# Adding the experts' weighted rows to the tokens' rows in HBM by accumulating indirect transfers, instead of storing them and gathering them back

## The chip, the cores and the metric

The kernel runs on one core of one Trainium2 chip. The metric is the device time of one execution in microseconds (us). All operands are float32.

## What is computed

Two layers of a gated decoder work on `x`, four sequences of 512 tokens with 512 features (2048 tokens). Each layer adds a state-space block and then a feed-forward block, both behind a tanh gate. The feed-forward block of the first layer is a mixture of 16 experts, of which each token takes 4, with weights. That block and how its rows meet again is what the change touches:

```python
x = x + tanh(g_xattn[0]) * ssm0(ctx, layernorm(x), ...)
x = x + tanh(g_ffn[0]) * moe(layernorm(x), ...)         # this block
x = x + tanh(g_xattn[1]) * ssm1(ctx, layernorm(x), ...)
x = x + tanh(g_ffn[1]) * lora_ffn(layernorm(x), ...)

def moe(x, ...):                       # x: 2048 tokens x 512
    w, sel = route(x)                  # 4 of 16 experts a token, weights sum to 2.5
    for each expert e:
        y = silu(x @ gate[e].T) * (x @ up[e].T) @ down[e].T      # inner size 256
        out += cw[:, e, None] * y      # cw is zero where e was not selected
    return out + shared_expert(x)
```

The scan of the state-space block reads only `ctx` and weights, not `x`; `x` enters it at the end, as the gate `silu(layernorm(x))`. So the scans of layer 2 can run while the experts of layer 1 are at work, and that is what the kernel does.

## The kernel before

**Stages.** The eight scans (two layers of four sequences) are stages s = 0 to 7. A stage has 32 units (16 states by two halves of the 512 channels). One unit is a multiplication on DVE (`mul_b`, L1498, which writes PSUM), a scan on DVE (`scan`, L1506), a multiplication by C on GpSimd (`mul_c`, L433) and a sum. In stages 0 to 4 TensorE sums the units in PSUM (L974). In stages 5 to 7 TensorE has the experts, and DVE sums (`add_y`, L1517), two units after the scan. `mul_c` of a unit starts only when `mul_b` of the next one is done, so that it lies beside the scan.

**Turns.** Stages 5 to 7 are cut into 48 turns of two units (an even and an odd one), and turn m carries one tile of tokens, with one lag for each step. The 8192 pairs of token and expert are sorted by expert into 79 chunks (`NCH`) of 128 rows. A tile has two chunks of the same expert or one: 32 full tiles and 15 half ones, 47 (`NTILE`). In turn m GpSimd issues the gathers of tile m + 2 after the even `mul_c` (`gather_rows`, L475, one indirect transfer of 128 rows of 2 KB for each chunk, from `xn_d`). SP issues the loads of the B and C rows (L293, 512 KB), the expert's weights of tile m + 1 (`load_tile_w`, L312, 1.5 MB; it first waits until tile m - 1 has left TensorE, as there are two slots) and the store of tile m - 1 (`store_tile`, L318) into `ys_d`, an array in HBM with a row for each pair. TensorE runs tile m - 1: the gate and up products (L1054), the next tile's transposes (L1033), the down product (L1065). ACT forms the tanh (L715) and copies the result out of PSUM (`tile_out`, L722) into the one buffer `YSB`, for which it waits on the store of the tile before. DVE forms the hidden rows (`tile_hidden`, L1524 and L1527) before `add_y` and before `scan` of the even unit.

**Routing.** In stage 4 DVE ranks the experts and works out each pair's slot (`slots`). Then eight rounds turn slots into an index of rows: ACT marks the row of each pair (`mark_rows`, L676 and L682), DVE marks its chunk (`mark_chunks`, L1490), and TensorE multiplies the marks (`index_round`, L1041), which leaves in PSUM, for each slot, the number of its token. DVE copies that to `IDX` (L1633). The slots, as integers (`SLU`), and the weights (`CWK`) are kept for the tail.

**Tail.** When the last unit is summed, GpSimd gathers the four expert rows of each token from `ys_d` (L520, 64 indirect transfers, 16 for each sequence b), and DVE adds them with their weights to `X` (`combine`, L1680, 16 instructions for each sequence). Then for each sequence: statistics (L1299), the gate (L627, L1309), transposes and the sum (L984, L1323), statistics again, the normalised rows (L636), their transposes (L993), the router of the second feed-forward (L1225), its gates on DVE (L1690 to L1716), the base product (L1195, three of four blocks ahead of the transposes L1208, one behind L984), the LoRA product (L1217) and the last sum (`lora_add`, L1725). Sequence b is begun before sequence b - 1 is finished: on DVE the order is combine(b), statistics(b), logits and gates of b - 1, gate and sum of b, `lora_add`(b - 1). GpSimd adds the bias of b - 1 (L510) meanwhile.

The waits that matter for the order stand in these lines:

```python
dve.wait_ge(gathered[q], 16 * TOPK * (b + 1))     # combine
pe.wait_ge(x_final, QT * l)                       # base(l, ...) behind lora_add(l - 1)
pool.wait_ge(ys_stored, 16 * NTILE)               # the tail's gathers behind all stores
```

## Time and profile before

| | |
|---|---|
| median of 3 runs | 1691.06 us (1689.95 to 1692.73) |
| the profiled execution | 1696.96 us, its span 1695.2 us |
| PE busy | 1259.6 us, 74% |
| PE weight loads | 694.2 us, 41% |
| DVE busy | 1498.9 us, 88% |
| ACT busy | 823.0 us, 49% |
| GpSimd busy | 874.9 us, 52% |
| DMA | 264.26 MB, of which 37.50 MB on GpSimd's queue |
| stages 5 to 7 with the tiles | about 915 to 1495 us |
| the tail | about 1495 us to the end |

Busy shares are means over stages with different limits, so the table alone does not say what a change is worth. Times in the rows are from the start of the span. "POOL" is GpSimd. A row of the timeline gives start, duration, engine, line, operation, output and input; in square brackets stands how long the engine had been idle and what ended that.

### The profile page before, as it was taken

Reading aid. Unit: us, or ns where it says so; the run is one execution under the profiler, and the core shown is the slowest. Engines: PE = TensorE matmul, PEld = TensorE weight load, DVE = VectorE, ACT = ScalarE, POOL = GpSimd, SP = SyncE. Lnnn points to the kernel's source line nnn. Section 1 sums busy time; section 2 is a strip of 40 time slices with the busy share of each in tenths; the row PEclk is TensorE's granted clock in tenths of the full one; section 3 lists DMA queues with packets and bytes.
Section 4 is the critical chain, followed back from the end, with each engine's and each line's share of the span. In section 5 each row is a group of like instructions: output and inputs, shape, how many; then the busy total and the mean of one; then the engine's idle time right before and its main releaser. Section 6 shows DMA issues by size and latency. Waiting matters only on the chain.

```text
span 1695.2 us, 13647 instructions
## 1 busy us (share of the span) xinstructions
PE 1259.6 (74%) x4084; PEld 694.2 (41%) x4084; DVE 1498.9 (88%) x1511; ACT 823.0 (49%) x1288; POOL 874.9 (52%) x449
## 2 busy tenths in 40 slices
PE   5566576677666876778777998789987899805678
PEld 2122132333233322334343656556665566603344
DVE  3999999899989999999987999899998999967883
ACT  4455537363725363532692666546665444404341
POOL 0357636643663367433245456764557666466521
PEclk7798789789978898898887999989999899956888
DMA  6244435523542354334155777766886788654421
GB/s 224 74 135 124 108 99 143 131 67 107 143 132 60 90 142 115 89 94 125 38 137 137 227 250 265 250 218 214 262 251 205 269 274 265 222 162 122 138 74 50
DMA packets 99834, 264.26 MB, mean 156 GB/s; under 512 B 10832, under 2 KB 11344, under 8 KB 93616
## 3 DMA queue, kind: packets, MB, share of 16 engines
q1 hardware_dynamic: 87936, 225.36, 44.3%
q0 software_dynamic: 11440, 37.50, 6.5%
q8 instruction: 33, 0.54, 0.1%
q10 hardware_dynamic: 384, 0.52, 0.1%
q14 instruction: 41, 0.34, 0.1%
HBM read 233.73 MB, written 29.62 MB: 155 GB/s over the span
## 4 chain that ended last, share of the span: by engine, by line
DVE 22%; PE 18%; issue 8%; DMA 5%; POOL 4%; ACT 4%; SPq 0%; DVEq 0%; ACTq 0%; POOLq 0%
PE banks L1054 8%; DVE state L1506 7%; DVE banks L1498 5%; PE banks L1065 3%; DMA expert_w<-in_moe_w 3%; POOL state L433 2%; DMA ys_d<-expert_out 2%; PE banks L1195 2%; DVE y_scan L1517 2%; DVE x_res L1680 1%; PE banks L1033 1%; DVE du L1265 1%; DVE small L1299 1%; PE banks L974 1%; PE banks L1225 1%
## 5 line engine op out<-in xcount | busy, mean ns | idle before, releaser
L433 POOL TENSOR_TENSOR state<-state,bc_rows 128x1024 f32<-128x1024 f32 x256 | 605.7, 2367 | 673.2 <-DVE banks L1498 673.1
L974 PE MATMUL banks<-state,ident 128*128 128x512 f32 x640 | 366.5, 706 | 194.2 <-POOL state L433 193.9
L1506 DVE TENSOR_TENSOR_SCAN state<-decay,banks 128x1024 f32<-128x1024 f32 x176 | 402.1, 2285 | 9.8 <-ACT decay L658 5.1
L1498 DVE TENSOR_TENSOR banks<-du,bc_rows 128x1024 f32<-128x1024 f32 x256 | 351.6, 1374 | 22.2 <-PE banks L974 8.2
L1054 PE MATMUL banks<-z_gate,expert_w 128*128 128x256 f32 (+1 forms) x1504 | 288.8, 351 | 12.0 <-DMA expert_w<-in_moe_w 6.7
L974 PEld LDWEIGHTS banks<-state,ident 128*128 128x128 f32 x640 | 127.1, 215 | 405.4 <-POOL state L433 289.9
L658 ACT ACTIVATE decay<-delta,neg_a 128x511 f32<-128x511 f32 x352 | 231.2, 713 | 104.8 <-DVE state L1506 51.8
L1054 PEld LDWEIGHTS banks<-z_gate,expert_w 128*128 128x128 f32 x1504 | 252.5, 193 | 67.2 <-issue 25.5
L1506 DVE TENSOR_TENSOR_SCAN state<-expert_w,banks 128x1024 f32<-128x1024 f32 x80 | 182.9, 2286 | 2.8
L1065 PE MATMUL banks<-expert_w,hidden 128*128 128x512 f32 x316 | 159.0, 619 | 2.9 <-DVE hidden L1527 2.9
L1517 DVE TENSOR_TENSOR y_scan<-y_scan,state 128x1024 f32<-128x1024 f32 x96 | 136.2, 1420 | 11.5 <-POOL state L433 11.5
L658 ACT ACTIVATE expert_w<-delta,neg_a 128x511 f32<-128x511 f32 x160 | 103.7, 710 | 15.3 <-DVE state L1506 15.3
L708 ACT ACTIVATE z_gate<-banks 128x512 f32<-128x512 f32 (+1 forms) x94 | 49.4, 526 | 75.8 <-PE banks L1033 74.7
L722 ACT ACTIVATE expert_out<-banks 128x512 f32<-128x512 f32 x79 | 45.5, 596 | 75.5 <-DMA ys_d<-expert_out 58.8
L1013 PE MATMUL banks<-y_scan,expert_w 128*128 128x512 f32 x128 | 68.2, 694 | 8.5 <-DVE hidden L1535 7.3
L1065 PEld LDWEIGHTS banks<-expert_w,hidden 128*128 128x128 f32 x316 | 54.8, 198 | 35.6 <-issue 31.7
L538 ACT ACTIVATE du<-banks,chan 128x512 f32<-128x512 f32 x32 | 23.9, 770 | 92.0 <-PE banks L919 90.7
L984 PE MATMUL banks<-ident,y_scan 128*128 128x128 f32 x128 | 23.6, 342 | 57.6 <-DVE y_scan L1309 52.7
L715 ACT ACTIVATE hidden<-banks 128x256 f32<-128x256 f32 (+1 forms) x94 | 32.3, 343 | 70.2 <-PE banks L1054 70.2
L1021 PE MATMUL banks<-expert_w,hidden 128*128 128x512 f32 x64 | 41.6, 811 | 31.0 <-DVE hidden L1535 31.0
L1195 PE MATMUL banks<-expert_w,du 128*128 128x512 f32 x128 | 58.3, 610 | 0.0
L646 ACT ACTIVATE rstd<-rstd 128x4 f32<-128x4 f32 x16 | 3.3, 205 | 106.3 <-DVE rstd L1304 78.5
(233 smaller groups left out, 1670.8 us busy)
## 6 DMA issues: line engine op xcount, KB each, us to landing
bc_rows<-bc_d SPq DMA_DIRECT2D x208, 512.0 KB, 4.9
expert_w<-in_moe_w SPq DMA_DIRECT2D x48, 1536.0 KB, 9.1
ys_d<-expert_out SPq DMA_DIRECT2D x32, 512.0 KB, 10.3
ctx_t<-in_ctxT SPq DMA_DIRECT2D x8, 512.0 KB, 6.7
x_res<-in_x SPq DMA_DIRECT2D x4, 1024.0 KB, 10.5
xn_d<-y_scan SPq DMA_DIRECT2D x4, 1024.0 KB, 7.5
ys_d<-expert_out SPq DMA_DIRECT2D x15, 256.0 KB, 9.2
out_x<-x_res SPq DMA_DIRECT2D x3, 1024.0 KB, 4.3
```

Of the source, the lines that this page charges most:

```text
L433: nc.gpsimd.tensor_tensor(W[:, c % 4], W[:, c % 4], bcast2(BC[:, u, 1, :]), ALU.mult).then_inc(mulc_done, 1)
L658: ins = nc.scalar.activation(DAS[c % n][:, m, 1:], DEL[:, s % 2, et, 1:], ACT.Exp, scale=AN[:, lay(s), et, state:state + 1])
L708: nc.scalar.activation(XST[:, 2 * h:2 * h + 2, 0:n], XT[:, h, :, 0:n], ACT.Copy).then_inc(xst_ready, 1)
L722: nc.scalar.activation(YSB[:, r, :], out_bank(j, r), ACT.Copy).then_inc(yev, 1)
L974: mm = nc.tensor.matmul(PS[:, m], ID[:, :], W[:, c % 4, m, :], start=False, stop=True, skip_group_check=True)
L1013: mm = nc.tensor.matmul(AUX[g], MW[:, 0, at:at + P], XNT[:, k, :], start=(k == 0), stop=(k == ET - 1))
L1054: mm = nc.tensor.matmul(PS[:, it, g * TILE:g * TILE + n], MW[:, u % 2, at:at + P], XST[:, k, 0:n], start=(k == 0), stop=(k == ET - 1))
L1065: mm = nc.tensor.matmul(out_bank(j, r), HT[:, u % 2, it, r * P:(r + 1) * P], MW[:, u % 2, at:at + D], start=(it == 0), stop=(it == IT - 1))
L1195: nc.tensor.matmul(PS[:, q], xnt[:, k, q * P:(q + 1) * P], BW[:, k, :], start=(k == 0), stop=(k == ET - 1))
L1498: nc.vector.tensor_tensor(drive(s), DU[:, s % 2, 2 * h:2 * h + 2, :], bcast2(BC[:, u, 0, :]), ALU.mult).then_inc(mulb_done, 1)
L1506: nc.vector.tensor_tensor_scan(flat(W[:, c % 4]), flat(DAS[c % da_slots(s, i)]), flat(drive(s)), 0.0, ALU.mult, ALU.add).then_inc(scan_don ...
L1517: nc.vector.tensor_tensor(y, y, W[:, k % 4], ALU.add).then_inc(w_free, 1)
```

## The change

In stages 5 to 7 each finished chunk of an expert is added to an array of the tokens' sums in HBM, and nothing is gathered in the tail.

- A new array `acc_d` in HBM holds `X` (after the shared expert's part) from before the tiles: SP stores each sequence into it (`store_sum`, 1 MB each, four of them, at the ends of stages 2 and 3 and twice in stage 4). `xn_d` and `acc_d` get 256 rows ahead of the tokens' (`SPARE`), filled from `x` at the start (two copies of 512 KB from HBM to HBM), so that empty slots have rows of their own to read and to add to.
- The index product also carries the weights: `mark_chunks` writes for each pair the chunk's mark and the mark times weight over row number, in four instructions instead of one, and the product has 158 columns instead of 79. `read_index` then copies the weights of the slots (`SLOTW`), gives empty slots a spare row (`PLACE`) and forms `IDX`.
- ACT scales each row by its slot's weight as it copies it from PSUM (`tile_out`), into one of two buffers in turn (`YSB` and the first two blocks of `X`, which are free once `X` is in `acc_d`). It waits for the additions of the tile two before, not for the store of the last.
- GpSimd issues `add_rows(m - 2)` after the odd `mul_c` of turn m: an indirect transfer with add for each chunk, from the buffer into `acc_d` at the rows of `IDX`. It first waits for ACT's copies and for all earlier additions to have landed (`added`). The store to `ys_d` is gone from SP's list.
- After the last unit GpSimd issues the additions of the last tile, and SP, when all 79 have landed, loads `acc_d` back into `X`: four loads of 256 KB for the first sequence, then one of 1 MB for each other. The 64 gathers and the 64 instructions of `combine` are gone.

```diff
-        GK = [W[:, 0:2].rearrange("p a b n -> p (a b) n"), W[:, 2:4].rearrange("p a b n -> p (a b) n"),
-              DA[:, :, :, :].rearrange("p a b n -> p (a b) n"),
-              MW[:, 1, 0:QT * D].rearrange("p (q n) -> p q n", q=QT)]
+        OUT = [YSB, X[:, 0:RT]]
...
-        xn_d = nc.dram_tensor("xn_d", (NB * L, D), F32, kind="Internal").ap()
-        ys_d = nc.dram_tensor("ys_d", (NCH * P, D), F32, kind="Internal").ap()
-        ys_c = ys_d.rearrange("(c p) n -> p c n", p=P)
-        xn_t = xn_d.rearrange("(b q p) n -> b p q n", p=P, q=QT)
+
+        xn_d = nc.dram_tensor("xn_d", (SPARE + NB * L, D), F32, kind="Internal").ap()
+        acc_d = nc.dram_tensor("acc_d", (SPARE + NB * L, D), F32, kind="Internal").ap()
+        xn_t, acc_t = [v[SPARE:, :].rearrange("(b q p) n -> b p q n", p=P, q=QT) for v in (xn_d, acc_d)]
...
+            def store_sum(b):
+
+                sp.wait_ge(shacc, QT * (b + 1))
+                sp.dma_start(acc_t[b], X[:, b * QT:(b + 1) * QT, :]).then_inc(acc_stored, 16)
...
+            for rows in (xn_d, acc_d):
+                sp.dma_start(rows[0:SPARE, :], t["x"][0, 0:SPARE, :]).then_inc(spare_stored, 16)
...
+                if s >= 2:
+                    store_sum(s - 2)
...
                     sp.dma_start(xn_t[NB - 1], XN).then_inc(xn_stored, 16)
+                    store_sum(NB - 2)
                 if k == HS - 4:
-                    sp.wait_ge(slots_ready, 2)
+                    store_sum(NB - 1)
+                    sp.wait_ge(slots_ready, 1)
...
-                    if m:
-                        store_tile(m - 1)
...
+            sp.wait_ge(added, 16 * NCH)
+            for q in range(QT):
+                sp.dma_start(X[:, q, :], acc_t[0][:, q, :]).then_inc(acc_first[q], 16)
+            for b in range(1, NB):
+                sp.dma_start(X[:, b * QT:(b + 1) * QT, :], acc_t[b]).then_inc(acc_in[b - 1], 16)
...
+            def add_rows(j):
+
+                pool.wait_ge(yev, DONE[j + 1])
+                if j:
+                    pool.wait_ge(added, 16 * DONE[j])
+                for r in range(BLOCKS[j]):
+                    at = chunk_of(j) + r
+                    nc.gpsimd.indirect_dma_start(
+                        out=acc_d, out_offset=bass.IndirectOffsetOnAxis(ap=IDX[:, at:at + 1], axis=0),
+                        in_=OUT[j % 2][:, r, :], in_offset=None, compute_op=ALU.add).then_inc(added, 16)
...
+                        if m == 0 and c == 0:
+                            pool.wait_ge(acc_stored, 16 * NB)
                         if c % 2 == 0 and m + 2 < NTILE:
                             gather_rows(m + 2)
+                        if c % 2 and m >= 2:
+                            add_rows(m - 2)
...
-            pool.wait_ge(w_free, HS * STAGES + PRE_W)
-            pool.wait_ge(ys_stored, 16 * NTILE)
-            for g in range(NT):
-                b, q = g // QT, g % QT
-                if b:
-                    pool.wait_ge(combined, TOPK * QT * (b - 1) + (TOPK - 1) * QT + q + 1)
-                for k in range(TOPK):
-                    nc.gpsimd.indirect_dma_start(
-                        out=GK[q][:, k, :], out_offset=None, in_=ys_d,
-                        in_offset=bass.IndirectOffsetOnAxis(ap=SLU[:, k, g:g + 1], axis=0)).then_inc(gathered[q], 16)
-                if q == QT - 1 and b:
-                    add_bias(b - 1)
-            add_bias(NB - 1)
+            add_rows(NTILE - 1)
+            for b in range(NB):
+                add_bias(b)
...
             def tile_out(j):
-                if j:
-                    act.wait_ge(ys_stored, j * 16)
+                if j >= 2:
+                    act.wait_ge(added, 16 * DONE[j - 1])
                 for r in range(BLOCKS[j]):
                     act.wait_ge(y_done, DONE[j] + r + 1)
-                    nc.scalar.activation(YSB[:, r, :], out_bank(j, r), ACT.Copy).then_inc(yev, 1)
+                    at = chunk_of(j) + r
+                    nc.scalar.activation(OUT[j % 2][:, r, :], out_bank(j, r), ACT.Copy, scale=SLOTW[:, at:at + 1]
+                                         ).then_inc(yev, 1)
...
-                    mm = nc.tensor.matmul(INDEX, ROWHOT[n % 3][:, c, :], CHUNKHOT[n % 3][:, c // TOPK, c % TOPK, :],
+                    mm = nc.tensor.matmul(INDEX, ROWHOT[n % 3][:, c, :], flat(CHUNKHOT[2 * (n % 3) + c // TOPK][:, c % TOPK]),
...
-                row = COUNT1[:, 0:NCH].unsqueeze(1).unsqueeze(1)
-                shape = [P, PPR // TOPK, TOPK, NCH]
-                nc.vector.tensor_tensor(CHUNKHOT[n % 3], row.to_broadcast(shape), own.unsqueeze(3).to_broadcast(shape),
-                                        ALU.is_equal).then_inc(chunkhot, 1)
+                row = COUNT1[:, 0:NCH].unsqueeze(1).to_broadcast([P, TOPK, NCH])
+                over_j = lambda v: v.unsqueeze(2).to_broadcast([P, TOPK, NCH])
+                of_group = lambda v, g: v.rearrange("p (k t) -> p t k", k=TOPK)[:, g, :]
+                for a in range(PPR // TOPK):
+                    hot, g = CHUNKHOT[2 * (n % 3) + a], PPR // TOPK * n + a
+                    ins = nc.vector.tensor_tensor(hot[:, :, 0, :], row, over_j(of_group(CHUNK1, g)), ALU.is_equal)
+                link(ins)
+                for a in range(PPR // TOPK):
+                    hot, g = CHUNKHOT[2 * (n % 3) + a], PPR // TOPK * n + a
+                    ins = nc.vector.tensor_tensor(hot[:, :, 1, :], hot[:, :, 0, :], over_j(of_group(SHARE, g)), ALU.mult)
+                ins.then_inc(chunkhot, 1)
+
+            def read_index():
+
+                dve.wait_ge(indexed, ROUNDS)
+                nc.vector.tensor_copy(SLOTW[:, :], INDEX[:, NCH:])
+                empty = T2[:, 0:NCH]
+                for r in range(RT):
+                    ins = nc.vector.tensor_scalar(empty[:, r::RT], INDEX[:, r:NCH:RT], 0.0, PLACE[:, r:r + 1], ALU.is_equal, ALU.mult)
+                link(ins)
+                nc.vector.tensor_tensor(IDX, empty, INDEX[:, 0:NCH], ALU.add).then_inc(index_ready, 1)
...
-                    combine(b)
+                    for landed in [acc_in[b - 1]] if b else acc_first:
+                        dve.wait_ge(landed, 16)
```

## Rows read from the trace of the kernel before

**Rows 1.** Busy time by stretch: us, busy time of each engine, TensorE's clock, DMA share, GB/s.
```profile
950.00:1100.00 150.00, 133.06 (x591) 93.30 (x589) 138.63 (x134) 92.24 (x153) 88.10 (x50) 0.98 0.73 248
...
1400.00:1450.00 50.00, 44.96 (x219) 33.54 (x218) 48.29 (x47) 24.56 (x48) 31.32 (x18) 1.00 0.84 272
```

**Rows 2.** What DVE waited for, 905 to 1495 us: us in total, times, longest.
```profile
DVE hidden L1524 <- ACT hidden L715: 18.5, 26, 2.2
DVE y_scan L1517 <- POOL state L433: 11.5, 10, 3.0
```

**Rows 3.** Timeline of stage 7, 1400 to 1450 us.
```profile
1401.91 2.37 POOL L433 TENSOR_TENSOR state<-state,bc_rows 128x1024 f32<-128x1024 f32 x1 [3.01 <-DVE banks L1498]
...
1407.51 2.36 POOL L433 TENSOR_TENSOR state<-state,bc_rows 128x1024 f32<-128x1024 f32 x1 [0.47 <-DVE banks L1498]
...
1413.14 2.35 POOL L433 TENSOR_TENSOR state<-state,bc_rows 128x1024 f32<-128x1024 f32 x1 [3.27 <-DVE banks L1498]
...
1415.73 1.22 DVE L1517 TENSOR_TENSOR y_scan<-y_scan,state 128x1024 f32<-128x1024 f32 x1
...
1422.42 0.36 SPq L312 DMA_DIRECT2D expert_w<-in_moe_w  x1
...
1432.55 7.07 PE L1054 MATMUL banks<-z_gate,expert_w 128*128 128x256 f32 x32
...
1436.62 0.42 DVE L1524 SCALAR_TENSOR_TENSOR hidden<-hidden,banks 128x256 f32<-128x256 f32 x1
```

**Rows 4.** Lines L475 (gathers: ns; then landing) and, last, L312 (weights: landing).
```profile
L475 POOL DMA_INDIRECT z_gate<-xn_d,selected x40: 946/983/2022, 893.9 to 1458.2; - x40
...
DMA to landing us min/median/max: 3.2/6.1/7.0
...
DMA to landing us min/median/max: 7.2/9.0/10.4
```

**Rows 5.** Timeline of the rounds in stage 4; last, from the tail's groups, a 256-element instruction.
```profile
842.50 0.93 DVE L1490 TENSOR_TENSOR expert_out<-expert_w,small 128x632 f32<-128x632 f32 x1
...
858.16 0.82 DVE L1490 TENSOR_TENSOR expert_out<-expert_w,small 128x632 f32<-128x632 f32 x1 [2.63 <-PE banks L1041]
...
878.32 2.29 DVE L1276 TENSOR_TENSOR softplus_tmp<-delta,softplus_tmp 128x2048 f32<-128x2048 f32 x1 [4.19 <-ACT softplus_tmp L584]
...
L1338 DVE TENSOR_TENSOR softplus_tmp<-small 128x256 f32<-128x256 f32 x4 | 1.7, 425 | 0.1
```

**Rows 6.** Timeline around the end of stage 7.
```profile
1488.30 4.64 POOL L433 TENSOR_TENSOR state<-state,bc_rows 128x1024 f32<-128x1024 f32 x2 [2.63 <-DVE banks L1498]
...
1494.62 0.72 ACT L887 ACTIVATE softplus_tmp<-softplus_tmp,tanh_gates 128x512 f32<-128x512 f32 x1 [8.61 <-DMA softplus_tmp<-in_base_b]
...
1525.92 0.21 ACT L646 ACTIVATE rstd<-rstd 128x4 f32<-128x4 f32 x1 [29.28 <-DVE rstd L1304]
```

**Rows 7.** Busy time from 10 to 20 us; then a row of the DMA issues.
```profile
10.00:20.00 10.00, 5.05 (x12) 1.90 (x10) 6.83 (x11) 3.90 (x9) 0.00 (x0) 1.00 1.00 353
...
out_x<-x_res SPq DMA_DIRECT2D x4, 256.0 KB, 2.2
```

**Rows 8.** Timeline of the tail, sequences 1 and 2.
```profile
1557.57 10.46 PE L1195 MATMUL banks<-expert_w,du 128*128 128x512 f32 x24
...
1571.59 1.09 PE L984 MATMUL banks<-ident,y_scan 128*128 128x128 f32 x8 [1.54 <-DVE y_scan L1309]
...
1583.62 5.68 DVE L1680 SCALAR_TENSOR_TENSOR x_res<-state,slot_w,x_res 128x512 f32<-128x512 f32 x2
...
1591.08 10.46 PE L1195 MATMUL banks<-expert_w,du 128*128 128x512 f32 x24
...
1601.61 0.30 DVE L1690 TENSOR_TENSOR small<-banks,router_b 128x16 f32<-128x16 f32 x2
...
1608.92 1.11 PE L1208 MATMUL banks<-ident,bc_rows 128*128 128x128 f32 x4 [7.38 <-DVE bc_rows L1716]
...
1611.12 4.00 PE L984 MATMUL banks<-ident,y_scan 128*128 128x128 f32 x16 [1.08 <-DVE y_scan L1309]
```

More of the change, by code:

```diff
@@ L1553, in _ @@
             link(nc.vector.reduce_sum(SM[:, 0, 0:1], T1[:, 0:P], AX.X))
[L1554 removed]
+            link(nc.vector.tensor_scalar(SM[:, 0, 1:2], SM[:, 0, 0:1], float(SPARE - P - 1), None, ALU.add))
+            for r in range(RT):
+                link(nc.vector.tensor_scalar(PLACE[:, r:r + 1], SM[:, 0, 0:1], float(r * P - 1), None, ALU.add))
             link(nc.vector.tensor_scalar(ROWID, COUNT1[:, 0:NT], float(P), SM[:, 0, 1:2], ALU.mult, ALU.add))
```

57 lines of the change are left out of this document (23 added, 34 removed).

## The prediction

> **What bounds the kernel now.** I read the busy times by stretch first, then what DVE waited for, then the timeline of one turn, and last the timeline of the tail. With the tiles DVE is busy 92% of a stretch and 97% of a late one [rows 1]. The DMA engines move 248 to 272 GB/s there. In stages 5 to 7 (580 us) DVE idles 18.5 us for ACT's tanh, which comes from TensorE, and 11.5 us for GpSimd's `mul_c` [rows 2]. So DVE's own list sets the length of a turn, about 11.2 us for a full tile (`mul_c` of two even units start at 1401.91 and 1413.14 [rows 3]) and a little less for a half one, and the other engines have small rooms beside it. These are read from the same turns. GpSimd: after the odd `mul_c`, which ends at 1409.87, it idles 3.27 us until the next; that `mul_c` ends at 1415.49 and DVE needs it at 1415.73, 0.24 us later. TensorE: weights issued at 1422.42 are needed at 1432.55, 10.1 us later, and DVE takes up the tile's tanh at 1436.62, within 0.1 us of its being ready. So neither engine may be much later. In the tail, the waits change from step to step, and it is read by its chain.
>
> **The tail, what is removed.** I go by sequence. T is the end of the `lora_add` of the round before.
>
> Sequences 2 and 3: at T = 1583.7 DVE starts `combine`. TensorE makes three base blocks from 1591.08 to 1601.54, then idles 7.38 us for DVE's gates and turns to L984 at 1611.12 [rows 8]. With `combine` gone (16 instructions, one pair of them stretched to 5.68 us beside GpSimd's bias) DVE has its statistics done by T + 3 and then waits for the router product, which ends as the base blocks begin (1591.1). From the logits to L1208 it needs 7.3 us (1601.61 to 1608.92 [rows 8]), the gate to L984 another 2.2 (1611.12): 1600.6. That is before 1601.54, so TensorE is next late: L984 can start at 1601.54 + 0.9 for L1208 = 1602.4. Saved: 1611.1 - 1602.4 = 8.7 us, twice 17.4. What comes behind (L984 to `lora_add`) stays.
>
> Sequence 1: the base blocks end at 1557.57 + 10.46 = 1568.03, L984 starts at 1571.59 [rows 8]. By the same working it can start at 1568.7. Saved: 2.9.
>
> Sequence 0: here waits take the place of waits. The last `mul_c` ends at 1492.94 [rows 6]. Then GpSimd adds tile 45 (two chunks, 2.4 us of issue), waits until they land, adds tile 46 (one chunk), and that must land. The trace shows no add. Its landing is bounded by an indirect gather's 3.2 to 7.0 us from its start [rows 4]; I take 5, since the queues are empty there but each row is read and written. 1492.9 + 1.4 + 5 + 5 = 1504.4. SP then issues the loads of 4 MB. **Behind them in SP's list stands the load of the base bias** (L398), and ACT's next instruction waits for it: it starts at 1494.62 as that load lands, although it was issued before [rows 6]. ACT's first `rstd`, at 1525.92, stands behind it. The loads with the bias are 4.46 MB. A stretch in which the DMA engines are busy all the time moves 353 GB/s [rows 7], so 12.6 us; a lone load or store of 256 KB lands in 2.2 us, of which 0.7 would be transfer, so 1.5 for the rest. The bias lands at 1504.9 + 12.6 + 1.5 = 1519.0; ACT's 0.72 and a table load of 1.28 follow, and `rstd` runs at 1521.0 instead of 1525.9. Saved: 4.9 (between 0 and 10 by both bounds of the landings). Without that load in its place it would be 14. Sum of the tail: 17.4 + 2.9 + 4.9 = 25.2.
>
> The Trainium skill (DMA: Bandwidth & Descriptors, Anatomy of one DMA) puts a GpSimd transfer at about 2.0 us plus its bytes over 436 GB/s, 2.6 us for 256 KB. With 2.6 for each of the two landings the tail would save another 4.8 us. The gathers' 3.2 us at the least [rows 4] contain 0.95 of issue, so the trace is near it in a quiet stretch and twice as far off in a loaded one.
>
> **The routing, what is added.** A round's marks are one instruction of 0.93 us on DVE and become four of half as many elements. 256 elements take 0.42 us, so 316 take about 0.5; four and the link between them are 2.2. Eight rounds: + 10 us. DVE idles in that stretch 2.63 us for TensorE and 4.19 us for ACT, whose own list of marks sets the pace [rows 5]. These 6.8 us take most of it; 3.4 remain, and 0.7 for `read_index`, which stands on DVE's list. I take + 4 (between + 1 and + 10, with no cover at all). The wider product costs TensorE some 2 us a round; DVE is the later one there. The spare copies at the start and the four stores of 1 MB lie ahead of B and C rows on SP's queue, but DVE's list of waits holds none for a load [rows 2]; nothing. ACT's scaled copies go into idle time: it is busy 92 of 150 us [rows 1].
>
> **The tiles, what is moved.** The store of 256 or 512 KB a turn leaves SP's queue, and the same bytes are added from GpSimd's.
>
> Issue: after the odd `mul_c` GpSimd now issues two transfers for a full tile (32 tiles). No row shows an accumulating one. A gather takes 0.95 to 2.0 us, mostly 0.98, with 0.3 between two [rows 4]. Two at 0.98: 0.14 + 0.98 + 0.3 + 0.95 = 2.4 of the 3.27 (2.6 in some turns), hidden. With one of 2.0 it is 3.4: 0.1 to 0.8 late, of which 0.24 and more is absorbed. Bounds: 0, and with both at 1.9 (a second descriptor for the row that is read) 4.2, some 0.9 late for each full tile, 29 us. I take 5, nearest to the gather's row.
>
> A rule speaks against this place. By the Trainium skill (DMA: Bandwidth & Descriptors, SWDGE vs HWDGE vs iDMA) GpSimd writes its descriptors into rings in SBUF, from which DVE locks it out in its two-port modes. The spread from 0.95 to 2.02 us of equal gathers [rows 4] agrees. If every add were held up so, it would be the upper bound above.
>
> Transfers: TensorE's weights land in 9.0 us in the median, 10.4 at most [rows 4], and are needed after 10.1. An add reads its row as well as writing it, so a turn moves 0.43 MB more (0.84 busy share becomes about 0.95), 1.2 us at 353 GB/s, and it is issued when the weights are. With that, weights land at 10.2, and behind a half tile (its turn is shorter, the need comes at about 9.6) TensorE is 0.6 late. 15 half tiles: 9 us; I take + 8 (between 0, if the store's leaving the queue makes up for it, and 15 times 1.7 = 25, if an add costs twice that time). A gain is bounded by the 18.5 us of DVE's idle time [rows 2], of which the store's leaving could return some.
>
> Landing: GpSimd waits, before a tile's adds, for those of the tile before, one turn ago. They have 11.2 - 1.3 = 9.9 us; a gather takes 6.1 in the median and 7.0 at most [rows 4]. Nothing, with 3 us to spare for the reading. Queued behind the waiting add stand `mul_c`, the gathers and, through `mul_c`, DVE's sum.
>
> **Sum.** - 25.2 + 4 + 5 + 8 = - 8.2 us. The profiled execution took 1696.96 us, so it would be 1688.8; against the median, 5.9 lower, 1683.
>
> **Rivals.**
> - *A: the issue of an add takes twice a gather's.* For it: a row must be named for reading and for writing; the room is 3 us. Against: nothing in the rows. 29 in place of 5: 1707, slower. It decides from 1.5 us for each add. 18%.
> - *B: an add lands later than 9.9 us.* Then GpSimd stands in each turn, and all behind it. For it: each row makes two trips to HBM, and twice a gather's 6.1 or 7.0 us would be 12 or 14. Each us too late costs 45 us; at 10.7, with 36, 1719. 11%.
> - *C: the weights come later by 2 us, not by 1.2.* 15 x 1.7 = 25 in place of 8: 1700. For it: TensorE's room is under 0.3 us. 14%.
> - *D: the tiles cost nothing.* The store's leaving makes up for the reading and the adds fit: 1691 - 25 + 4 = 1670. 12%.
>
> That additions are lost or rows not combined isn't a rival for the time.
>
> **How the numbers follow.** The forecast has 45%, with its own range from 1668 to 1696. The whole range is 1660 to 1720: it takes in C and A, most of D, and B up to its stated size. About 0.2% is what a measurement can tell here, so faster ends at 1687.7 and slower begins at 1694.4. Faster: 0.37 of the forecast's share, D's 0.12, 0.01 of C: 0.5. Slower: A 0.17, B 0.11, C 0.10, 0.02 of the forecast: 0.4. The same: 0.1.
>
> **What would show it.** In the profile after: L984 of sequences 2 and 3 follows L1195's three blocks without 7 us of idle time, and the tail's period falls from 40 to 31 us. ACT's L887 waits for the base bias until about 25 us after the last `mul_c`. The adds' durations on GpSimd and their landing decide A and B; DVE's idle time for `mul_c` (11.5 now) and for ACT's tanh (18.5 now) would grow by 5 and 8 in the forecast. DVE's stretch from 840 to 900 us would be 4 us longer. I am wrong if an add's issue exceeds 1.5 us, if its landing exceeds 9.9 us, or if the base bias isn't late.

## The result, and the profile after

The changed kernel takes 2011.76 us (median of 4 runs, 2006.97 to 2018.74) where the kernel before takes 1691.51 beside it (1689.95 to 1692.73): a ratio of 1.190, with a 95% interval of 1.186 to 1.194. It is slower by 320 us, far outside the range of 1660 to 1720. The profiled execution took 2010.22 us, its span 2008.5. Marks are read from one profiled execution of each kernel, and that of before (1696.96 us) was 5.5 us above its median, so a difference of a few us between two of them is not safe.

Three marks cut the span into the parts of the prediction: S, where ScalarE's 128x1024 copy of `y_scan` opens stage 5; M, the end of the last `mul_c`; E, the end of the span.

| us | S | M | E | S to M, the tiles | M to E, the tail |
|---|---|---|---|---|---|
| before | 914.6 | 1492.9 | 1695.2 | 578.3 | 202.3 |
| after | 915.5 | 1833.2 | 2008.5 | 917.7 | 175.3 |
| difference | + 0.9 | | + 313.3 | + 339.4 | - 27.0 |

The tail gained what was forecast (27.0 for 25.2). Stage 4, which holds the routing, took 100.7 us (814.8 to 915.5) for 100.6 before (814.0 to 914.6): the routing cost 0.1 us instead of 4. **All of the loss is in the stretch with the tiles**, which I had put at + 13. The windows of after that answer to [rows 1] (us, busy time of PE, weight loads, DVE, ACT and GpSimd with the number of instructions, then granted clock, DMA share, GB/s):

```profile
950.00:1100.00 150.00, 97.62 (x370) 64.02 (x369) 82.81 (x83) 53.37 (x89) 72.51 (x41) 0.83 0.52 154
1400.00:1450.00 50.00, 32.32 (x123) 21.80 (x124) 31.29 (x30) 20.05 (x36) 26.19 (x14) 0.80 0.49 136
```

DVE falls from 92 and 97% busy to 55 and 63%, and no engine takes its place: all five and the DMA engines do less. So it is a chain of waits. The waits of after, 950 to 1750 us (who waited, for whom, us in total, times, longest):

```profile
POOL state L445 <- DVE banks L1538: 346.8, 51, 12.8
DVE hidden L1564 <- ACT hidden L733: 342.0, 46, 12.6
PE banks L1055 <- DVE hidden L1567: 300.0, 44, 12.6
ACT expert_out L741 <- DMA acc_d<-expert_out,selected: 226.7, 20, 14.9
ACT x_res L741 <- DMA acc_d<-x_res,selected: 200.4, 19, 13.7
```

GpSimd waits for DVE, DVE for ACT's tanh, and ACT for the additions: 427 us in 39 listed waits, 11 us each (over the whole execution 479 us in 44). In [rows 2] DVE's wait for ACT's tanh was 18.5 us. The end of the ring is ACT's L741, the scaled copy out of the banks, which the prediction let pass. The page's shares of the chain that ended last say the same:

```profile
DMA acc_d<-expert_out,selected 11%; DMA acc_d<-x_res,selected 10%; POOL state L445 5%; DVE banks L1538 5%; POOL acc_d L498 3%; DVE state L1546 3%; ACT decay L676 3%; DVE y_scan L1557 3%; PE banks L1217 2%; PE banks L1076 1%; PE banks L1247 1%; DVE hidden L1564 1%; PE banks L996 1%; DVE small L1321 1%; ACT L676 1%
```

One turn of the timeline of after (start, duration, engine, line, operation, and in brackets the idle time and what ended it), to be held against [rows 3]:

```profile
1301.66 2.35 POOL L445 TENSOR_TENSOR state<-state,bc_rows 128x1024 f32<-128x1024 f32 x1 [7.04 <-DVE banks L1538]
1304.16 1.63 POOL L498 DMA_INDIRECT acc_d<-x_res,selected  x1 [0.15 <-issue]
1306.10 2.36 POOL L498 DMA_INDIRECT acc_d<-x_res,selected  x1 [0.30 <-issue]
1307.92 2.93 POOL L445 TENSOR_TENSOR state<-state,bc_rows 128x1024 f32<-128x1024 f32 x1
...
1317.24 0.69 ACT L741 ACTIVATE x_res<-banks,slot_w 128x512 f32<-128x512 f32 x1 [12.81 <-DMA acc_d<-x_res,selected]
1317.95 1.28 ACT L676 ACT_TABLE_LOAD   x1
1319.24 1.33 ACT L676 ACTIVATE decay<-delta,neg_a 128x511 f32<-128x511 f32 x2
...
1321.14 0.37 ACT L733 ACTIVATE hidden<-banks 128x256 f32<-128x256 f32 x1
...
1321.54 0.42 DVE L1564 SCALAR_TENSOR_TENSOR hidden<-hidden,banks 128x256 f32<-128x256 f32 x1 [9.99 <-ACT hidden L733]
...
1324.85 2.34 POOL L445 TENSOR_TENSOR state<-state,bc_rows 128x1024 f32<-128x1024 f32 x1 [12.81 <-DVE banks L1538]
1327.35 1.59 POOL L498 DMA_INDIRECT acc_d<-expert_out,selected  x1 [0.16 <-issue]
```

With two output buffers ACT's copy of tile j needs the additions of tile j-2. GpSimd issues these at 1304.16 and 1306.10, and ACT has been waiting for them since 1304.43. Behind ACT's wait stand its decays and the next tile's tanh, behind the tanh DVE, behind DVE the next `mul_c`, and behind that `mul_c` the next addition, at 1327.35. **The wait closes a ring**: one turn is 23.2 us from addition to addition, where it was about 11.2.

### The profile page after: what moved, and what is told of

The parts are those of the page before. It is cut to its first block, busy times and chain, and to the rows that moved or that the text cites. A ratio compares the mean times of both kernels' runs of the same rounds, so it can differ in the third digit from the quotient of the medians.

```text
span 2008.5 us, 13640 instructions
## 1 busy us (share of the span) xinstructions
PE 1331.4 (66%) x4084; PEld 728.3 (36%) x4084; DVE 1447.2 (72%) x1476; ACT 821.5 (41%) x1288; POOL 947.3 (47%) x464
## 4 chain that ended last, share of the span: by engine, by line
DMA 21%; DVE 16%; ACT 9%; POOL 8%; PE 8%; issue 6%; DVEq 0%; SPq 0%; ACTq 0%; POOLq 0%
DMA acc_d<-expert_out,selected 11%; DMA acc_d<-x_res,selected 10%; POOL state L445 5%; DVE banks L1538 5%; POOL acc_d L498 3%; DVE state L1546 3%; ACT decay L676 3%; DVE y_scan L1557 3%; PE banks L1217 2%; PE banks L1076 1%; PE banks L1247 1%; DVE hidden L1564 1%; PE banks L996 1%; DVE small L1321 1%; ACT L676 1%
## 5 line engine op out<-in xcount | busy, mean ns | idle before, releaser
L445 POOL TENSOR_TENSOR state<-state,bc_rows 128x1024 f32<-128x1024 f32 x256 | 622.3, 2434 | 853.3 <-DVE banks L1538 853.2
L1564 DVE SCALAR_TENSOR_TENSOR hidden<-hidden,banks 128x256 f32<-128x256 f32 (+1 forms) x94 | 35.3, 376 | 374.0 <-ACT hidden L733 374.0
L996 PEld LDWEIGHTS banks<-state,ident 128*128 128x128 f32 x640 | 128.6, 219 | 404.2 <-POOL state L445 290.8
L1055 PE MATMUL banks<-ident,z_gate 128*128 128x128 f32 x160 | 39.9, 388 | 175.5 <-DVE hidden L1567 174.3
L741 ACT ACTIVATE expert_out<-banks,slot_w 128x512 f32<-128x512 f32 x40 | 25.8, 684 | 260.8 <-DMA acc_d<-expert_out,selected 260.4
L741 ACT ACTIVATE x_res<-banks,slot_w 128x512 f32<-128x512 f32 x39 | 25.3, 684 | 219.7 <-DMA acc_d<-x_res,selected 218.7
L1055 PEld LDWEIGHTS banks<-ident,z_gate 128*128 128x128 f32 x160 | 27.5, 202 | 210.2 <-issue 208.1
L1087 PEld LDWEIGHTS banks<-expert_w,hidden 128*128 128x128 f32 x316 | 75.9, 272 | 54.1 <-issue 47.7
L498 POOL DMA_INDIRECT acc_d<-expert_out,selected x40 | 77.1, 1927 | 12.8 <-issue 8.3
L498 POOL DMA_INDIRECT acc_d<-x_res,selected x39 | 74.3, 1906 | 10.3 <-issue 7.5
L538 POOL TENSOR_TENSOR x_res<-x_res,softplus_tmp 128x2048 f32<-128x2048 f32 x4 | 18.1, 4531 | 122.3 <-ACT delta L654 122.3
## 6 DMA issues: line engine op xcount, KB each, us to landing
x_res<-acc_d SPq DMA_DIRECT2D x3, 1024.0 KB, 10.1
```

What stands on the lines that cost most here:

```text
L445: nc.gpsimd.tensor_tensor(W[:, c % 4], W[:, c % 4], bcast2(BC[:, u, 1, :]), ALU.mult).then_inc(mulc_done, 1)
L498: nc.gpsimd.indirect_dma_start(out=acc_d, out_offset=bass.IndirectOffsetOnAxis(ap=IDX[:, at:at + 1], axis=0), in_=OUT[j % 2][:, r, :], in_ ...
L741: nc.scalar.activation(OUT[j % 2][:, r, :], out_bank(j, r), ACT.Copy, scale=SLOTW[:, at:at + 1]).then_inc(yev, 1)
L996: mm = nc.tensor.matmul(PS[:, m], ID[:, :], W[:, c % 4, m, :], start=False, stop=True, skip_group_check=True)
L1055: mm = nc.tensor.transpose(XT[:, h, k, r * P:(r + 1) * P], rows_of(j)[:, r, at:at + P], ID[:, :])
L1087: mm = nc.tensor.matmul(out_bank(j, r), HT[:, u % 2, it, r * P:(r + 1) * P], MW[:, u % 2, at:at + D], start=(it == 0), stop=(it == IT - 1))
```

## The experiments

Runs of the kernel before beside them had medians of 1688.31 us (e1 to e4), 1689.53 (e5 to e8), 1691.08 (e9 to e12) and 1690.47 (e13 and e14). e1 and e4 are single executions; the others are medians of four, e10 of ten. There are 47 tiles and 79 additions; where an expectation says 39 turns or 78 additions, it went by the listed waits and a slip of counting. In the expectations M is the theory that the ring above makes the loss. L is its second form: the lead of an addition, the time from its start until ScalarE's copy could begin, decides. I is the theory that what is left then is GpSimd's time.

**e1, no additions.** GpSimd only counts the semaphore up; the experts are left out of the sums.

```
-                if j:
-                    pool.wait_ge(added, 16 * DONE[j])
-                for r in range(BLOCKS[j]):
...
+                pool.sem_inc(added, 16 * BLOCKS[j])
```

> The changed kernel with the 79 accumulating transfers left out (the experts' rows are not added to the sums; all else, the routing of weights, ACT's scaled copies and the loads of the sums, stays). Theory M (all of the loss is the waiting for additions, above all ACT's wait for the additions of the tile two before, with the next tile's tanh and the decays queued behind it on ACT): the stretch with the tiles is as before, about 578 us from the first transposes to the last mul_c, and the tail keeps its 27 us: 1665 us. Rival R (the rest of the change costs something in the turns, through ACT's scaled copies into X or GpSimd's order): over 1690 us.

1646.6 us, span 1644.9. S to M is 571.6 us, the tail 160.2. All of the loss comes with the additions; scaled copies, marks, stores of the tokens' rows cost nothing there. The time is 18 us below the 1665 expected: the tail has no landing to wait for (160.2 us, 175.3 in the change), and the stretch is 6.7 us shorter than before. ACT's 58.8 us of waits for the stores of `ys_d` are gone too, but they can explain little of it: the loops of e8 and e12 below keep these stores and 60 us of such waits and take 573.6 and 574.6 us. The rest may be the difference between single executions.

**e2, four buffers.** ACT writes to four buffers in turn and needs the additions of tile j-4. (As the buffers reach into the second sequence of `X`, ACT waits once, ahead of the tiles, for all four stored sums in place of one.)

```
-        OUT = [YSB, X[:, 0:RT]]
+        OUT = [YSB] + [X[:, RT * i:RT * (i + 1)] for i in range(3)]
...
-                    act.wait_ge(added, 16 * DONE[j - 1])
+                    act.wait_ge(added, 16 * DONE[j - 3])
```

> The changed kernel with four output buffers instead of two, so that ACT waits for the additions of the tile four before. GpSimd still waits for the additions of the tile before. Theory M: ACT's wait (479 us of idle time) goes. What remains is GpSimd's own loop, an issue of about 4.2 us and a landing of about 9 for a full tile, 13 us, against DVE's 11.2: the 47 turns take between 590 and 640 us, the kernel 1680 to 1730, I say 1700. Theory T (the additions' issue time and their traffic are what costs, and ACT's wait only shows it): GpSimd or the weights are late all the same, over 1850 us.

1720.91 us, ratio 1.019 (1.017 to 1.021): 291 us of the 320 are gone, with the same additions in the same places. Their landing took 9.8 us in the median (4.6 to 11.6). S to M is 627.2.

**e3, and the base bias first.** The load of `base_b` moves ahead of SP's wait for the additions.

> As the run before, with the load of the base bias put ahead of the wait for the additions on SP's queue. In the changed kernel's trace the statistics of sequence 0 are ready at 1858.1 us and ACT's rstd starts at 1865.5, behind that load. If the bias is what it waited for: 7 us less than the run before (5 to 9). If the loads of the sums hold it instead: no difference.

1713.58 us, ratio 1.015 (1.013 to 1.017): 7.3 us less than e2, all of it in the tail (176.1 to 168.5; the tiles' 627.8 stay).

**e4, plain writes, two buffers.** The changed kernel without `compute_op=ALU.add`: the same rows are overwritten, not added to.

> The changed kernel, two buffers, with plain indirect writes instead of accumulating ones (a row keeps the last expert's values only, so the sums are not formed). The waits stay. Theory M: the loop of a turn is issue + landing + about 10 us on ACT, DVE and GpSimd; a plain write needs less of the first (about 1 us instead of 1.6 to 2.7 each) and lands somewhat sooner, 7 to 9 us from its start: 18 to 21 us a turn, 1850 to 1920 us in all. Theory A (it is the reading and adding that makes it slow, a plain write would fit into the turn): below 1720 us.

1898.78 us. Without any adding the ring is there too: ACT's L741 waits 379.5 us in 44 waits for these writes (479.1 in 44 for the additions), which land 6.7 us after their start in the median. So it isn't the adding that closes it. It sets how long a turn is: S to M 809.9 for 917.7.

**e5, the additions one turn earlier**, two buffers as in the change.

```
-                        if c % 2 and m >= 2:
-                            add_rows(m - 2)
+                        if c % 2 and m >= 1:
+                            add_rows(m - 1)
...
-            add_rows(NTILE - 1)
```

> The changed kernel, two buffers kept, but GpSimd issues tile m-1's additions in its turn m instead of tile m-2's: one whole turn earlier, and the loop has no addition left behind it. Theory L (lead): the cost of the change is that ScalarE's copy of tile j needs tile j-2's additions landed, and these were issued at the very moment the copy was due. One turn earlier gives a lead of about 11.5 us against 3 to 4 us of issue of two additions and 4.6 to 11.6 us of landing (median 9.8 in the run with four buffers), together 13 to 14 us: 1 to 3 us of waiting a turn stay, over 39 turns 40 to 110 us on top of the 1721 us of four buffers, less some 8 us because the last tile's additions leave earlier. About 1770 us, 1720 to 1840. Rival (writes out of X's rows, or additions as such, hold ScalarE up whatever their time of issue): it stays over 1900 us.

1712.4 us, ratio 1.014 (1.012 to 1.015): no further buffer is needed. Theory L holds, but I expected 1770, and 1712.4 is below the range of 1720 to 1840. ACT's wait was 1.4 us in each of 25 listed. It fell into ACT's idle time (the stretch, 626.9 us, is no longer than with four buffers); I had put each us of it on the path.

```profile
L498 POOL DMA_INDIRECT acc_d<-expert_out,selected x39: 1573/1627/2672, 947.9 to 1545.2; - x39
L498 POOL DMA_INDIRECT acc_d<-x_res,selected x39: 1570/1978/2619, 959.2 to 1536.2; - x39
...
DMA to landing us min/median/max: 4.8/10.1/11.6
```

These rows (ns at the least, in the median, at most; then the landing in us) also decide two bounds of the prediction: an addition takes 1.6 to 2.0 us of GpSimd, and it lands 10.1 us after its start.

**e9, half a turn earlier**: `add_rows(m - 2)` behind the even product instead of the odd one.

> The changed kernel, two buffers, tile m-2's additions in GpSimd's turn m as in the change, but after the turn's first product instead of its second: half a turn (5.6 us) earlier, a dose between the change (2012 us) and one whole turn earlier (1712 us). Theory L (lead): ScalarE's copy then waits about 5.5 us less than the 11 a turn of the change, and the loop loses 7.7 - 5.6 = 2 us a turn or nothing, over 39 turns 0 to 80 us, on top of 1720 us (1712 and the 8 us by which the last tile's additions leave later): 1790 us, 1720 to 1840. Rival (what helped in the run with the whole turn was not the lead but that the additions stood behind another product or gather): it stays over 1900 us.

1746.45 us, ratio 1.033 (1.031 to 1.035), in the range, 44 us better than its middle. The dose (lead: median from an addition's start to where the copy that needs it stood ready; waits over the stretch S to M, ACT's over the execution):

| place of the additions | lead, us | S to M, us | ACT's waits for additions, and mean | DVE's waits for ACT's tanh, us | DVE's waits for `mul_c`, us |
|---|---|---|---|---|---|
| the change | 0.0 | 917.7 | 44, 10.9 us | 374.0 | 2.8 |
| half a turn earlier (e9) | 4.9 | 660.4 | 35, 2.6 us | 5.9 | 106.7 |
| one turn earlier (e5) | 11.1 | 626.9 | 25, 1.4 us | 27.4 | 53.4 |
| four buffers (e3) | 23.7 | 627.8 | 7, 0.4 us | 33.8 | 51.0 |

Half a turn took 8.3 us off the mean wait, and of this only 4.9 are lead. The rest is landing: from the start of a tile's last addition to the end of ACT's wait it is 9.9 us in the median in the change, 5.9 in e9 and 10.2 in e5. In the change and in e5 the load of a tile's weights (1.5 MB) is mostly issued within 2 us of that addition, before or behind it; in e9 it is issued 5.8 us ahead of it in the median. That this makes the difference is likely, not shown.

The lead is shown as the cause of the ring: half a turn of it takes DVE's waits for the tanh from 374.0 to 5.9 us. What e9's stretch takes more than e5's, 33.5 us, isn't that ring. There additions and gathers stand behind the same product, the odd `mul_c` is late and DVE waits for it. Rows of e9, 905 to 1500 us and one of its turns:

```profile
DVE y_scan L1557 <- POOL state L445: 95.6, 35, 6.1
DVE hidden L1564 <- ACT hidden L733: 5.9, 6, 1.9
...
1392.56 1.59 POOL L498 DMA_INDIRECT acc_d<-x_res,selected  x1 [0.15 <-issue]
1394.46 1.71 POOL L487 DMA_INDIRECT ctx_t<-xn_d,selected  x1 [0.30 <-issue]
1396.48 0.97 POOL L487 DMA_INDIRECT ctx_t<-xn_d,selected  x1 [0.30 <-issue]
1397.47 2.36 POOL L445 TENSOR_TENSOR state<-state,bc_rows 128x1024 f32<-128x1024 f32 x1
...
1399.86 1.23 DVE L1557 TENSOR_TENSOR y_scan<-y_scan,state 128x1024 f32<-128x1024 f32 x1 [1.61 <-POOL state L445]
```

From one turn on, more lead brings nothing.

**e6, one turn earlier, four buffers, the bias first.**

> Four buffers, base_b's load ahead of the wait for the additions (1713.6 us), and the additions one turn earlier as well. Theory L: the tiles' stretch (627.8 us) stays as it is, since four buffers already gave ScalarE the lead, and only the tail becomes shorter, as the last tile's additions are issued a turn earlier: 6 to 10 us. 1705 us, 1700 to 1711. Rival: the additions' own wait for the tile before (GpSimd) was costing, and moving them changes it: 1690 or less, or above 1715.

1706.39 us, ratio 1.010 (1.008 to 1.012). S to M 627.9, the tail 162.8 for e3's 168.5.

So about 56 us stay (627.9 against 571.6 in e1) whatever the lead. The rest of the runs ask what they are.

**e7, as e3 but plain writes** (rows overwritten, not added to).

> The 1713.6 us kernel with the accumulation taken out of its indirect writes (they overwrite the rows instead of adding to them; all else is the same). It tells what adding costs apart from the lead. Theory I (issue): the 50 us by which the tiles' stretch stays longer than before are GpSimd's: 78 additions at 1.97 us against 1.19 us for a plain indirect write in the run with two buffers, 0.78 x 78 = 61 us of GpSimd's time, most of it on the path: the stretch falls from 628 to about 585 us, the time to 1673 us (1660 to 1690). Rival (traffic: these rows move once more either way, or GpSimd's wait for landing): over 1700 us.

1672.21 us, ratio 0.990 (0.988 to 0.992), as expected. S to M is 591.3: plain writes cost 20 us over e1, adding another 36.5. Their issue is 1.33 us in the mean (median 1.03), an addition's in e3 2.00 (median 1.95).

**e10, as e6 with half rows** (the experts are left out of the sums that the tail loads).

> The 1706.4 us kernel (four buffers, additions a turn earlier, base_b's load early) whose additions carry the first 256 columns of each row alone, 1 KB for 2 KB, into an array of half the width that the tail doesn't read: the experts' outputs are left out of the sums, four small stores come in while the routing runs. As many additions, as many rows, half the bytes. If an addition costs GpSimd its 2.0 us by the rows it describes, its issue stays at 1.9 to 2.0 us and the tiles' stretch at 628 us: 1706 us (1698 to 1712), though the landing falls below 8 us. If issue or stretch go by bytes, issue falls towards 1.3 to 1.5 us, as for the plain write, and the time to 1665 to 1685 us.

1694.36 us, ratio 1.003 (1.001 to 1.004), 4 us below the range of the first theory and 9 above that of the second. The issue stayed at 1.99 us in the mean, 1.97 for whole rows in e6: from 1 to 2 KB it goes by rows, not by bytes. S to M is 617.2: of the 56 us some 11 went with the bytes, 46 stayed.

**e11, products on GpSimd in place of the additions** (experts left out).

> The changed kernel without its additions (1646.6 us; the sums lack the experts), but with a product of 128x1024 numbers on GpSimd into unused rows in place of each, 78 of them at 2.36 us, where an addition is 2.0 us and 0.3 us of issue before it. No transfer is in it. Theory I: the 56 us that additions with enough lead add to the tiles' stretch (571.6 to 627.8 us) are GpSimd's time and nothing else: the stretch comes to 627 us and the time to 1702 us (1692 to 1712). Rival (traffic of the additions slows weights and the others): the stretch stays at 572 to 600 us, the time at 1646 to 1675 us.

1805.56 us, ratio 1.068 (1.066 to 1.071): above both theories, and it can't tell them apart. Timeline of it:

```profile
1379.27 3.33 POOL L497 TENSOR_TENSOR x_res<-x_res 128x1024 f32<-128x1024 f32 x1
1382.56 3.33 POOL L461 TENSOR_TENSOR softplus_tmp<-softplus_tmp,y_scan 128x1024 f32<-128x1024 f32 x1
...
1377.40 2.99 DVE L1555 TENSOR_TENSOR y_scan<-y_scan,state 128x1024 f32<-128x1024 f32 x1
1380.31 3.38 DVE L1536 TENSOR_TENSOR banks<-du,bc_rows 128x1024 f32<-128x1024 f32 x1
...
1389.57 1.22 DVE L1555 TENSOR_TENSOR y_scan<-y_scan,state 128x1024 f32<-128x1024 f32 x1
```

DVE's operations on two operands of SBUF take 2.99 to 3.38 us beside GpSimd's product, 1.22 without it, and the product 3.33 for 2.36. My stand-in took more than time. Over the stretch DVE is busy 687.7 us for 539.6 in e1 and idle 32.1 for 32.0, so all of the 148 us more are DVE's own longer instructions (ACT waited 220.6 us for the products, and none of it reached DVE). This agrees with the Trainium skill (SBUF — State Buffer, Summary: rules for kernel authors): a DVE operation with two inputs in SBUF and a GpSimd operation that reads SBUF exclude each other, and the second to issue waits. DVE's scans stayed at 2.28 us beside them.

**e13 and e14, narrow gathers in place of the additions** (experts left out): two, or one, of 64 B a row for each addition; ScalarE doesn't wait for them.

> The changed kernel without its additions, as in the 1646.6 us run (the sums lack the experts), and in the place of each addition two indirect gathers of 64 B a row, 128 rows each, into rows that nobody reads; ScalarE doesn't wait for them. 156 of them, 0.98 us and 0.30 of issue each by the gathers of the trace: 200 us of GpSimd, about the 179 us that 78 additions take at 2.0 and 0.3, with 1.3 MB of traffic in all instead of 40 MB read, added and written back. Theory I (GpSimd's time): the tiles' stretch goes from 571.6 to 620 to 640 us, the time to about 1704 us (1690 to 1715). Rival (traffic and landing of the additions): the stretch stays under 595 us, the time under 1672 us.

> The same with one narrow gather in the place of each addition, 78 of them, 100 us of GpSimd's time. Theory I, with the slack that GpSimd shows (217 us idle over the stretch, in pieces of 2.6 us before a product): the first 100 us mostly fit in it and cost little, and the price rises from there, as 78 plain indirect writes (127 us) cost 20 us and 78 additions (179 us) cost 56. Stretch 580 us, 573 to 590; time 1656 us, 1647 to 1668. If the price is proportional to GpSimd's time it is half of the other run's, 28 us and more.

| in each addition's place | their time, count x mean us | GpSimd busy, us | S to M, us | DVE idle, us | DVE waits for `mul_c`, us |
|---|---|---|---|---|---|
| nothing (e1) | 0 | 341 | 571.6 | 32.0 | 12.4 |
| one narrow gather (e14) | 79 x 1.22 = 96 | 442 | 579.4 | 47.1 | 12.8 |
| plain write (e7) | 79 x 1.33 = 105 | 453 | 591.3 | 58.3 | 22.6 |
| addition (e6) | 79 x 1.97 = 156 | 517 | 627.9 | 88.5 | 53.4 |
| two narrow gathers (e13) | 158 x 1.12 = 177 | 531 | 637.5 | 99.5 | 51.8 |

e14 took 1664.61 us, ratio 0.985 (0.982 to 0.987), as expected; e13 took 1727.45, 1.023 (1.019 to 1.026), its stretch as expected and its time 12 above the range. With next to no traffic the stretch grows as it does with additions: 96 us of narrow gathers cost 8, 177 cost 66. Between the two, 156 us would cost 51 by a straight line, and additions cost 56. GpSimd's busy time over the stretch, which also holds the longer rows of the gathers and of `mul_c` beside them, is the better measure: 101 us more cost 8, 190 more cost 66, so 176 more would cost 57. DVE's idle time grows from 32.0 to 88.5 us in e6, which is all of the 56: 41 of it are waits for `mul_c`, 16 waits for ACT's tanh, whose cause is not shown. **The 56 us are GpSimd's time**, for the most part: the gaps between its products (217 us in e1) take up the first 100 us, and then it is late for DVE. Plain writes (113 us more of busy time cost 20, where the line gives 15) lie a little above the line. What half the bytes give back is 11 us at most (e10). In e6, 916 to 1484 us, GpSimd is busy 470 of 568 us, DVE 488; in e1 340 and 537:

```profile
916.00:1484.00 568.00, 474.61 (x2018) 329.92 (x2019) 488.35 (x459) 295.63 (x497) 470.43 (x239) 0.94 0.75 224
```

**e8, accumulating gathers in the tail alone.** The loop keeps the stores of before (with ScalarE's weights). In the tail sequences 0 and 1 are gathered and summed by DVE, 2 and 3 by accumulating gathers straight into their rows, each row's four behind one another:

```
+                    if k:
+                        pool.wait_ge(summed[b, q], 16 * k)
+                    nc.gpsimd.indirect_dma_start(
+                        out=X[:, g, :], out_offset=None, in_=ys_d,
+                        in_offset=bass.IndirectOffsetOnAxis(ap=SLU[:, k, g:g + 1], axis=0),
+                        compute_op=ALU.add).then_inc(summed[b, q], 16)
```

> The kernel before with ScalarE's weighting kept (store_tile by SyncE and one buffer as before, no additions in the loop), and in the tail the tokens of sequences 0 and 1 gathered and summed by VectorE as before, those of sequences 2 and 3 summed by accumulating gathers straight into their rows in the core's memory, 32 of them, issued by GpSimd between the others. Expected: routing +1 us as measured, tiles' stretch 578 us as before, VectorE loses two combinations of the tail that were worth 8.7 us each, 17.4 us, and GpSimd, with 32 additions at 1.6 us and 0.3 between them beside 32 gathers at 1.25, is done about 116 us after the last step of the loop, where sequence 3 is wanted at 105 to 110: 0 to 12 us given back. 1677 us, 1668 to 1690. If additions at the tail issue at 2 us and more, or land late one behind the other, it comes out no better than before (1688).

1677.63 us, ratio 0.992 (0.990 to 0.994): **faster than both kernels**, by 0.8% over the kernel before, little but clear of the noise. S to M 573.6; the tail 185.2 for 202.3, 17 less for the 17.4 that two combinations were put at in [rows 8]. By the medians the kernel gained 11.9 us; the 17 may hold some of what the profiled execution of before had above its median.

**e12, two of sequence 1's four terms as well.**

> The 1677.6 us kernel (sequences 2 and 3 summed by accumulating gathers in the tail), and of sequence 1's four terms a token two come by accumulating gathers as well, two by VectorE. VectorE's combination of sequence 1, 13 us in which only two waits of 3 us fall, is halved: 6.5 us less on the path. GpSimd issues 8 more additions at 1.85 us for 8 fewer gathers at 1.25, 5 us more, where it is done 13 us before VectorE wants the last rows. 1671 us, 1667 to 1677; 1680 or more if sequence 1's additions land after VectorE comes to them, as they start only when sequence 0's gathers have been issued.

1671.43 us, ratio 0.989 (0.986 to 0.991), the best version here. The rows of its additions (as above) show what they take in the quiet tail: 1.55 us of issue, 5.8 of landing, where the loop has 1.6 to 2.0 and 10.1:

```profile
L546 POOL DMA_INDIRECT x_res<-ys_d,slots x40: 1541/1550/2810, 1517.1 to 1609.3; - x40
...
DMA to landing us min/median/max: 4.8/5.8/6.4
```

## Why the prediction was wrong, point by point

**The step that failed is "ACT's scaled copies go into idle time: it is busy 92 of 150 us" [rows 1].** It took a share of busy time for an answer to a question of order, and so it put ACT's new wait at nothing without a reason. The copy was given this wait, for an addition, and I asked only for GpSimd's wait before an addition ("They have 9.9 us"), which was indeed harmless: 4.4 us in all in the change, 2.3 in e5. The trace of before had the answer. In [rows 3] GpSimd's odd `mul_c` ends at 1409.87, the place of the addition. ACT's copy, in a row of the same turn that the prediction doesn't use (before, same columns), stood ready 2.54 us ahead of its start, at 1409.78:

```profile
1412.32 1.08 ACT L722 ACTIVATE expert_out<-banks 128x512 f32<-128x512 f32 x2 [2.54 <-DMA ys_d<-expert_out]
1414.52 0.27 ACT L715 ACTIVATE hidden<-banks 128x128 f32<-128x128 f32 x1
```

So the addition is issued when its landing is wanted. The lead is 0 (and measured 0.0 in the change), the landing at least 3.2 us by [rows 4], and behind the copy and two decays stands the tanh that DVE takes, in the turn of [rows 3], within 0.1 us of its being ready. The check to make is this: for each wait that a change adds, when is it released, when is it asked for, and what stands behind it. Of the + 339.4 us of the stretch this step is 290.8 (917.7 to 626.9 in e5). The other 48.6 are the next point. With + 0.9 ahead of S and - 27.0 in the tail that is the + 313.3 measured, where the forecast had - 8.2.

**Issue: + 5, bounds 0 to 29; measured + 48.6** (626.9 us in e5 for 578.3 before; 55.3 over the 571.6 of e1). The term was mis-sized. An addition takes 1.6 to 2.0 us in the median, not a gather's 0.98. Rival A had the mechanism and nearly the size (two at 1.9); one pair in e6 shows what it missed:

```profile
1411.54 2.58 POOL L498 DMA_INDIRECT acc_d<-x_res,selected  x1 [0.19 <-issue]
1414.43 1.57 POOL L498 DMA_INDIRECT acc_d<-x_res,selected  x1 [0.31 <-issue]
```

With the idle time before them that is 4.65 us in all, which is also the mean of the 32 pairs, for the 3.27 us of room [rows 3]: 1.4 us late in each of 32 full tiles, 44 us. So an estimate from the pairs leaves 5 of the 48.6 us open.

**Transfers: + 8; not there as forecast.** TensorE's listed waits for weights, its own and those of the weight loads, are 9.6 us in e5 and were 21.9 in before. The turns had become longer; that this is why the weights were in time isn't tested by itself.

**Landing: "Nothing, with 3 us to spare".** Additions land in 10.1 us, the room was 9.9, so two of the signs that I had named came up (an issue over 1.5 us, a landing over 9.9). But rival B had the wait in the wrong place, GpSimd's own.

**The tail: - 25.2; measured - 27.0, by parts less well.** By the starts of each sequence's transposes on TensorE (L984, then L1006):

```profile
1873.90 3.87 PE L1006 MATMUL banks<-ident,y_scan 128*128 128x128 f32 x16 [49.90 <-DVE y_scan L1331]
...
1896.61 10.46 PE L1217 MATMUL banks<-expert_w,du 128*128 128x512 f32 x24
1907.35 1.04 PE L1006 MATMUL banks<-ident,y_scan 128*128 128x128 f32 x8
...
1926.05 10.46 PE L1217 MATMUL banks<-expert_w,du 128*128 128x512 f32 x24
1936.78 1.04 PE L1006 MATMUL banks<-ident,y_scan 128*128 128x128 f32 x8
...
1958.03 10.46 PE L1217 MATMUL banks<-expert_w,du 128*128 128x512 f32 x24
1968.76 1.04 PE L1006 MATMUL banks<-ident,y_scan 128*128 128x128 f32 x8
```

L1006 follows the base blocks within 0.3 us, as forecast, where [rows 8] has 7.38 us of idle time. The periods are 33.5, 29.4 and 32.0 us; before they were 37.2, 39.5 and 39.9. Saved: 3.8, 10.1 and 7.9 for 2.9, 8.7 and 8.7. Sequence 0 saved 0.7 for 4.9:

```profile
1843.11 1.58 POOL L498 DMA_INDIRECT acc_d<-expert_out,selected  x1 [4.38 <-DMA acc_d<-x_res,selected]
1847.79 1.76 SPq L406 DMA_DIRECT2D x_res<-acc_d  x4
...
1854.93 2.47 DVE L1321 BATCH_NORM_STATS2 small<-x_res 128x6 f32<-128x512 f32 x4 [19.53 <-DMA x_res<-acc_d]
...
1863.44 0.72 ACT L909 ACTIVATE softplus_tmp<-softplus_tmp,tanh_gates 128x512 f32<-128x512 f32 x1 [28.33 <-DMA softplus_tmp<-in_base_b]
```

The loads begin 14.6 us behind M for 11.5 forecast, and the bias lands 15.6 us behind them for 14.1 (the working goes from 1504.4 to 1504.9 there without a term for it); each was right in kind, and e3 shows what the load's place costs, 7.3 us. The last 4.5 us came from behind the last transposes (44.2 to 39.7 us) and were not forecast: TensorE's granted clock over them was 0.99 (1965 to 2008 us), 0.87 before (1650 to 1695 us), so it was at 2.4 GHz nearly all of that time. The same instructions took 40.8 us at 0.96 in e1 and 42.3 at 0.92 in e9. That the sum of the tail came within 2 us is in part luck: it was 4.2 us too high for sequence 0, and 4.5 that I hadn't forecast came at the end.

**Routing: + 4, measured + 0.1 over stage 4.** The marks' 10 us were covered by DVE's idle time better than I allowed. The other 0.8 us of S arose ahead of stage 4; S lies between 913.1 and 918.5 us in the runs e1 to e14.

The estimate that I weighed from the Trainium skill (DMA: Bandwidth & Descriptors, Anatomy of one DMA), 2.6 us for a transfer of 256 KB from GpSimd, is far under what an addition took: 4.8 us at the least, 10.1 in the median under load (e5).

## What to carry to other kernels

For each wait that a change adds, write down when it is released and when it is asked for, in the turns of the loop, and then what stands behind the waiting instruction in its own engine's list. A ring (engine A waits for a transfer that is issued behind B, and B waits for A) costs its whole latency in each turn, and lead cures it without a further buffer: one turn here. Where the earlier issue goes counts too: behind the other product it met the gathers and cost 33 us more (e9). An accumulating indirect transfer saves a combination only where its issuing engine has time: in the loop it cost 56 us beside a nearly full GpSimd, in the tail it saved 20 (1671.43 us in e12, 1691.08 before).

## What the hardware showed beyond expectation

- An accumulating indirect transfer of 128 rows takes GpSimd 1.57 us at the least (e5; 1.54 into SBUF, e12), a plain one 0.97 (e7), a gather 0.95 [rows 4]; half the bytes changed nothing (e10). It lands 10.1 us after its start in the loop (e5), a plain write 9.0 in its place (e7), an accumulating gather in the quiet tail 5.8 (e12).
- DVE's 128x1024 operation with both operands in SBUF goes from 1.22 to 3.4 us beside a GpSimd product, and that product from 2.36 to 3.33 (e11).
- How fast an addition lands depends on its place in the turn: 5.9 us to the end of ACT's wait in e9, 9.9 in the change and 10.2 in e5, where the 1.5 MB of weights are mostly issued within 2 us of it. No run tests the weights' part in this by itself.
